# Tiled attention scores, tops and masks on 64 by 128 row halves in place of 64 by 64 quarters, with a new order of all steps

## What is computed

```python
# layer 0
x = x + full_attention(layernorm(x))         # 16 heads of 8, no mask, softmax over all 1024 keys
x = x + ffn(layernorm(x))                    # 128 -> 512 -> 128, relu
h = normed(x)
h = h + causal_attention(rmsnorm(h))         # "causal": 16 heads of 8, 4 kv heads, latent k and v
h = h + local_attention(rmsnorm(h))          # "local": window of 32, 16 heads of 8, 4 kv heads
x = x + h
x = x + ffn(layernorm(x))
# layer 1
x = x + window_attention(layernorm(x))       # "padded": band of 32, 16 heads of 8, 2 kv heads
x = x + moe(x)                               # 8 experts of 352, best 2 of each token
x = x + sink_attention(layernorm(x))         # "sink": 8 heads of 16, window 128 and 4 sinks
x = x + moe(x)
```

## Time and profile before

| | |
|---|---|
| median of 3 runs | 2473.16 us (2466.74 to 2474.1) |
| profiled execution | 2472.5 us, span 2470.7 us |
| PE busy | 2166.9 us (88%), 25853 matmul records |
| DVE, ACT, POOL busy | 1653.9, 1440.0, 661.4 us |
| granted TensorE clock, mean | 0.947 |

### The profile page before, as it was taken

How to read it: one execution, slowest core, us unless ns; L and a number is a source line. 1 busy time by engine, 2 the same in 40 slices (tenths; PEclk the granted TensorE clock), 3 DMA queues, 4 the chain that set the end, 5 groups by cost and what they waited for, 6 DMA issues and landing times.

```text
span 2470.7 us, 61917 instructions
## 1 busy us (share of the span) xinstructions
PE 2166.9 (88%) x25853; PEld 1229.8 (50%) x25874; DVE 1653.9 (67%) x3651; ACT 1440.0 (58%) x2121; POOL 661.4 (27%) x597
## 2 busy tenths in 40 slices
PE   5588898789988999999898998899989889989987
PEld 2111231133322433423565446767857788766886
DVE  7888788776688777413745357675667576676545
ACT  1177657667887578799665774455344334344432
POOL 2400010020010202011233333433435364233563
PEclk8599999899999999999999999999999899989999
DMA  5600100111011111111222135535334666324576
GB/s 163 232 15 29 40 13 17 40 47 31 25 51 50 52 32 54 31 50 31 66 74 72 22 103 153 153 88 156 117 84 122 208 208 194 95 85 125 175 231 208
DMA packets 156238, 231.06 MB, mean 94 GB/s; under 512 B 19504, under 2 KB 79408, under 8 KB 155704
## 3 DMA queue, kind: packets, MB, share of 16 engines
q1 hardware_dynamic: 140952, 202.69, 28.1%
q0 software_dynamic: 9984, 20.73, 2.4%
q10 hardware_dynamic: 5024, 3.67, 0.6%
HBM read 152.17 MB, written 75.40 MB: 92 GB/s over the span
## 4 chain that ended last, share of the span: by engine, by line
PE 50%; DVE 19%; DMA 11%; ACT 7%; issue 6%; POOL 4%; SPq 3%; ACTq 0%; DVEq 0%; POOLq 0%
PE PS L1139 11%; DVE MS L1532 11%; PE PS L1188 6%; PE PS L1122 6%; ACT PT L1295 6%; PE PS L1102 5%; DMA scr_y<-XN,SL 3%; PE PS L1205 3%; PE PS L1089 3%; PE PS L1001 2%; PE PS L1011 2%; PE PS L972 2%; DMA WB<-in_mW 2%; PE PS L1082 2%; POOL scr_y L1756 2%
## 5 line engine op out<-in xcount | busy, mean ns | idle before, releaser
L1295 ACT ACTIVATE PT<-PS 128x1024 f32<-128x1024 f32 (+3 forms) x1216 | 1026.8, 908 | 399.5 <-PE PS L1122 392.0
L1532 DVE TENSOR_REDUCE MS<-PS 128x2 f32<-128x1024 f32 (+4 forms) x736 | 787.8, 1099 | 236.1 <-PE PS L1102 232.7
L1139 PE MATMUL PS<-PT,VA 128*9 128x512 f32 (+9 forms) x6720 | 571.3, 438 | 8.0 <-ACT PT L1295 6.2
L1122 PE MATMUL PS<-QO,KO 51*64 51x512 bf16 (+11 forms) x6304 | 444.4, 311 | 44.9 <-ACT PT L1295 16.1
L1102 PE MATMUL PS<-KO,QO 48*64 48x512 bf16 (+2 forms) x3520 | 302.9, 340 | 84.0 <-DVE MS L1532 70.8
L1122 PEld LDWEIGHTS PS<-QO,KO 51*64 51x64 bf16 (+3 forms) x6304 | 185.8, 107 | 238.7 <-ACT PT L1295 84.8
L1188 PE MATMUL PS<-SG,WB 128*128 128x128 f32 x2208 | 286.7, 283 | 16.8 <-DMA WB<-in_mW 14.4
L1102 PEld LDWEIGHTS PS<-KO,QO 48*64 48x64 bf16 (+1 forms) x3520 | 131.5, 107 | 337.4 <-DVE MS L1532 186.4
L1188 PEld LDWEIGHTS PS<-SG,WB 128*128 128x128 f32 x2208 | 269.1, 197 | 24.9 <-DMA WB<-in_mW 16.5
L1764 POOL DMA_INDIRECT scr_o<-SG,TO x184 | 181.5, 986 | 248.8 <-ACT SG L1337 226.0
L1317 ACT ACTIVATE HM<-PS 128x384 f32<-128x384 f32 x184 | 90.2, 490 | 224.9 <-PE PS L1188 224.9
(11 more groups left out here) (166 smaller groups left out, 2377.1 us busy)
## 6 DMA issues: line engine op xcount, KB each, us to landing
WB<-in_mW SPq DMA_DIRECT2D x184, 384.0 KB, 3.8
PT<-scr_y SPq DMA_DIRECT2D x40, 264.0 KB, 4.0
PT<-scr_o SPq DMA_DIRECT2D x16, 512.0 KB, 5.9
KO<-scr_k_full SPq DMA_DIRECT2D x32, 204.0 KB
QO<-scr_q_full SPq DMA_DIRECT2D x32, 192.0 KB
QO<-scr_q_causal SPq DMA_DIRECT2D x32, 192.0 KB
QO<-scr_q_local SPq DMA_DIRECT2D x32, 192.0 KB
QO<-scr_q_padded SPq DMA_DIRECT2D x32, 192.0 KB
```

Of the source, the lines that this page charges most:

```text
L1122: p = mm(pb[c:c + n, h2, at:at + tn], k[:, k0 + c:k0 + c + n], q[:, t0:t0 + tn], start=not masked, stop=True, skip_group_check=masked)
L1139: p = mm(bank[32 * h:32 * h + D + 1, c0:c0 + tn], va[0:kn, :], pt[0:kn, h % 2, at:at + tn], start=s["first"] and j == 0, stop=s["last"] an ...
L1295: e = activation(pt[0:r, :, a:b], ps[0:r, :, a:b], ACT.Exp, scale=s["A"].scale)
L1532: v.tensor_reduce(to, got, AX.X, ALU.max).then_inc(S["top"], 1)
```

## The change

The tiled attentions get two matmuls of 64 rows by 128 columns for each block, one for each head, in place of four quarters. A mask piece keeps four matmuls, but each is 64 rows by 128 columns: the identity table is 192 columns wide with ones at column i + 64, so that its columns 64 to 191 put the 64 mask rows into output rows 0 to 63 and its columns 0 to 127 put them into rows 64 to 127. `score_mms` charges two matmuls for a tiled mask, the mode is called "rows", and LEADS, URGENT, SHORT and WORTH have new values, which re-orders all queues. The chained scatters stay.

```diff
-LEADS = dict(full=(1132, -776, 406, -1439), ffn1=(-3117, -525, 2830, 2001), causal=(1089, -1943, -1344, -1890), local=(-1543, 777, -158, 647), ffn2=(-197, 3580, -615, -1022), padded=(-948, -510, -413, -182), moe1=(2339, -1699, 271, -906), sink=(556, 567, -1777, 1297), moe2=(2401, -2034, -4275, -134))
+LEADS = dict(full=(-137, -569, -272, -180), ffn1=(-1778, -830, -716, -282), causal=(1304, 385, -1379, 73), local=(1244, 123, 93, 3856), ffn2=(2516, 2107, -891, 386), padded=(1048, 664, -6, 196), moe1=(-858, -362, -27, -925), sink=(-110, -64, 517, 569), moe2=(1974, -667, -460, -1725))
...
-SHORT = dict(pe=2339.0, act=1281.0, dve=653.0, pool=2521.0, sp=24300.0)
+SHORT = dict(pe=2471.0, act=1359.0, dve=869.0, pool=5270.0, sp=9931.0)
 ISSUE = 500.0
-SWITCH, WORTH = 95.0, 285706.0
+SWITCH, WORTH = 95.0, 10298.0
...
-    return sum((1 if tiled else 2) * mm16(n) for n in blocks) + (1 if tiled else 2) * mm16(masked) * bool(masked)
+    return sum((1 if tiled else 2) * mm16(n) for n in blocks) + 2 * mm16(masked) * bool(masked)
...
-    return ("quarters", "quarters") if tiled else ("whole", "whole")
+    return ("rows", "rows") if tiled else ("whole", "whole")
...
-                    for c in range(2):
+                    for back in (64, 0):
                         for h2 in range(2):
-                            r, off = slice(64 * h2, 64 * h2 + 64), c0 + 64 * (1 - c)
-                            rows = C[m[0]][r, off:off + width].unsqueeze(1).broadcast_to([64, copies, width])
-                            mm(pb[64 * c:64 * c + 64, h2, at:at + copies * width], C["identw"][r, :], rows, start=i == 0, stop=False, skip_group_check=True)
+                            r = slice(64 * h2, 64 * h2 + 64)
+                            rows = C[m[0]][r, back + c0:back + c0 + width].unsqueeze(1).broadcast_to([64, copies, width])
+                            mm(pb[:, h2, at:at + copies * width], C["identw"][r, back:back + 128], rows, start=i == 0 and back == 64, stop=False,
+                               skip_group_check=True)
...
-                n = 64 if A.tiled else 128
                 for tt, at, k0, kn in s["part"]["blocks"]:
-                    for c in range(0, 128, n):
-                        for h2 in range(2):
-                            q, k = q_rows(A, U, 2 * s["hp"] + h2, A.K), k_rows(A, U, 2 * s["hp"] + h2, A.K)
-                            p = mm(pb[c:c + n, h2, at:at + kn], q[:, 128 * tt + c:128 * tt + c + n], k[:, k0:k0 + kn], start=not masked, stop=True,
-                                   skip_group_check=masked)
+                    for h2 in range(2):
+                        q, k = q_rows(A, U, 2 * s["hp"] + h2, A.K), k_rows(A, U, 2 * s["hp"] + h2, A.K)
+                        p = mm(pb[:, h2, at:at + kn], q[:, 128 * tt:128 * tt + 128], k[:, k0:k0 + kn], start=not masked, stop=True,
+                               skip_group_check=masked)
...
-                    n = min(kn, 64) if A.tiled else kn
-                    for c in range(0, kn, n):
-                        for h2 in range(2):
-                            q, k = q_rows(A, U, 2 * hp + h2, A.rows), k_rows(A, U, 2 * hp + h2, A.rows)
-                            p = mm(pb[c:c + n, h2, at:at + tn], k[:, k0 + c:k0 + c + n], q[:, t0:t0 + tn], start=not masked, stop=True,
-                                   skip_group_check=masked)
+                    for h2 in range(2):
+                        q, k = q_rows(A, U, 2 * hp + h2, A.rows), k_rows(A, U, 2 * hp + h2, A.rows)
+                        p = mm(pb[0:kn, h2, at:at + tn], k[:, k0:k0 + kn], q[:, t0:t0 + tn], start=not masked, stop=True,
+                               skip_group_check=masked)
...
-        "ident": np.eye(128, dtype=np.float32), "identb": bf16(np.eye(128)), "identw": bf16(np.tile(np.eye(64), (2, 1))),
+        "ident": np.eye(128, dtype=np.float32), "identb": bf16(np.eye(128)), "identw": bf16(np.tile(np.eye(64, 192, 64), (2, 1))),
```

## The result

The changed kernel takes 2506.87 us (median, 2502.99 to 2510.39) against 2473.36 us: 1.0141 of the kernel before, 95% interval [1.0117, 1.0165], so 33.5 us slower. A second series of runs gave 1.0145 [1.0127, 1.0163]. The forecast was 2523 us, slower.

The account below looks back on a forecast made before the run. PE was taken as the bound in the masked stretches (92% busy). Masks +50 us, with scores, loads, changes of tiling and order at 0, gave 2473.2 + 50 = 2523 us; range 2435 to 2590 us.

Parts of the forecast that it names:

- Masks, two passes: Tiled mask matmuls (L1089) on PE: a second pass of 68 us, 34 to 64 us on the path, taken as +50 us.
- Scores, quarters to halves: Tiled scores and tops on PE: one pass as before, fewer instructions worth at most 15 us, taken as 0.
- Loads of a pair: Two 128-column weight loads on PE overlap and hide behind the pass; bound 0 to +90 us, taken as 0.
- changes of tiling: PE switching tilings: row halves cost about 0.1 us per change like the others; bound -68 to 0, taken as 0.
- rivals 4 and 5: 4: a pair's 128-column loads don't overlap, 2590 us, chance 0.06; 5: changing into row halves is cheaper, 2455 us, 0.05.
- The rule of the Trainium skill: Column tiling disables fast weight load, so row halves would load faster than quarters; -68 us if loads set the tiling-change cost.
- The order: Re-ordered queues on all engines: the mix of batches may move +-60 us, no row gives the sign, taken as 0.
- More changes of tiling: New order on PE: WORTH falls from 286 to 10 us, so more tiling changes are likely, bounded at +-19 us.
- Rival 2: Whole kernel: the new order loses as well, +50 for masks and +60 for order, 2583 us; chance 0.14.
- rival 3: Masked stretches: ACT and DVE hold banks in hand, hiding the second mask pass; PE work +68 us, time 2475 us; chance 0.08.

## Why the prediction was right or wrong

**Masks, two passes: the mechanism right, the term too large.** The passes are there (0.41 us for 0.23), and the extra pass costs 21 us when it is added alone, not 50. The step that failed is the share on the path. It was read from PE's busy share of 92% and the chain's 64 us in L1089. Busy time says that a matmul is in flight, not that the array is full, and a chain shows where the time was, not what more work would cost: the added pass partly filled stretches that were empty and partly raised the clock.

**Scores, quarters to halves, taken at 0: wrong by some 20 us.** Three blocks of 160 columns take the same 0.21 us, but each load and each first group of a step is 12 to 14 ns shorter. The prediction compared the load of 107 ns with the untiled one of 103 and left the difference out. Together with the mask term the tiling costs 1.5 us, not 50. How far the loads alone make the 20 us is open.

**Loads of a pair, changes of tiling: right.** It is 0.21 us for three blocks and 0.1 us for each change, so rivals 4 and 5 fall. The rule of the Trainium skill, weighed against the earlier trace rows, agrees with the shorter load (12 ns); the change of tiling costs what it did.

**The order, taken at 0: wrong, and it is where the time went.** It costs 20 us with quarters and 33 us with row halves. The prediction's bound of +-60 us held, and so did its warning that the order was the weakest step. More changes of tiling, the one part of the order that it could bound, did not come. Rival 2 (the order loses as well, 2583 us) had the order's sign right, with 60 us for it where 20 to 33 were measured and 50 for the masks.

**So the forecast came out in its range by luck: two errors partly cancel.** It put the tiling edit at +50 us, where it is 1.5 in the old order and 13 in the new one, and the order at 0, where it is 20 to 33. It is right that the kernel gets slower, by 33.5 us, and wrong that the masks do it. The time of rival 3 (the pass is hidden, 2475 us) is that of the tiling edit in the old order, but by another way: the pass is not hidden, since it costs 21 us when it is added alone, and a saving of the same size stands against it.

Open: which placements of the new order make its 16 us more of empty time, why row halves fill less of it there than in the old order (the 13 us), and which of LEADS, URGENT, SHORT and WORTH is to blame. No run took the new order apart, by stage or by constant.

## What to carry to other kernels

When a change comes with a new schedule, run both halves of it: old order with new matmuls and new order with old ones. Here the half that could be worked out line by line cost 1.5 us in the old order and 13 in the new one, and the half that could not cost 20 to 33. More work on an engine that is "92% busy" can be cheap when part of it lands in its gaps: a pass of 68 us cost 21. So before a pass is priced at its length, count the empty time of its stretch. And a wait of some microseconds on PE can cost more than itself, because what follows runs at the lower clock; filler gives some of that back only where it ends before the wait does, so look in the trace for an idle gap behind every filling.

## What the hardware showed that was not expected

- More PE work raised the mean granted clock: 0.936, 0.947, 0.958 for no, one and two mask passes in the same order. A pass of 64 to 68 us cost 12 to 22 us of time.
- An empty stretch of 4.65 us was followed by matmuls at 1.2 GHz (granted clock 0.50, product 1.89 us for 1.04). With 17 matmuls of 512 columns in that wait the clock stayed at 2.4 GHz (1.00), and 33.5 us of such filler in 17 waits made the changed kernel 20 us faster.
- A bf16 weight load of 48 rows by 128 columns took 94 ns, one of 48 rows by 64 columns 106 ns.
- A change between 64 by 64 and 64 by 128 tiles cost 0.1 us (scores 0.33 us after a mask piece and not 0.23), like the other changes of tiling in these traces.
